# Attention on one core: the softmax sums turned by a third transposition instead of a product with a picking matrix

## The reference

```
a = layernorm(x) @ w_qkv                    # q, k, v of 16 heads, 32 numbers each
scores[q, k] = (q * 32**-0.5) . k           # windows of 128 queries; keys of the window before,
                                            # the same and the next (384; at a sequence's ends 256)
attn = softmax(scores)                      # over the keys
x = x + layernorm(attn @ v)
x = x + layernorm(ffn(layernorm(x)))        # ffn's weights: a base and 8 experts mixed per batch by a gate
```

## Time and profile before

| | |
|---|---|
| median of three runs | 2935.83 us (2935.25 to 2944.34) |
| profiled execution, its own time | 2944.44 us |
| its span, first to last instruction | 2942.7 us |
| mean granted TensorE clock | 0.993 of full speed |
| attention loop's first and last transposition of outputs | 586.2 us, 1301.4 us |
| one round of eight steps (turn of the maxima at 666.04 to that at 709.43) | 43.4 us |

### The profile page before, as it was taken

One profiled execution on the slowest core, in us unless ns is written; L12 is line 12 of the kernel. 1 busy time (PEld: TensorE's weight loads), 2 busy tenths in 40 slices (PEclk: granted clock), 3 DMA queues, 4 the chain that ended last, 5 costly groups with the idle time before them and its releaser, 6 DMA issues.

```text
span 2942.7 us, 55697 instructions
## 1 busy us (share of the span) xinstructions
PE 2878.3 (98%) x20380; PEld 2399.2 (82%) x20380; DVE 1994.3 (68%) x3769; ACT 1733.9 (59%) x3385; POOL 856.6 (29%) x715
## 2 busy tenths in 40 slices
PE   8999999999999999989989999999999999999998
PEld 6888888788888888777867888888888888888886
DVE  5333333488888887778868766886769766786664
ACT  3222222367776766666546666766667666686666
POOL 1000000188888887874400000400005000040003
PEclk9999999999999999999999999999999999999999
DMA  6554555688788879959998866986769765895642
GB/s 215 185 171 171 186 188 193 215 193 197 191 199 197 196 193 219 220 167 393 400 389 327 295 208 221 348 324 204 245 212 404 272 204 201 287 390 201 233 136 86
DMA packets 361430, 697.11 MB, mean 237 GB/s; under 512 B 26576, under 2 KB 127056, under 8 KB 361184
## 3 DMA queue, kind: packets, MB, share of 16 engines
q1 hardware_dynamic: 335456, 629.63, 66.8%
q10 hardware_dynamic: 17424, 32.24, 3.1%
q0 software_dynamic: 8304, 31.98, 2.7%
HBM read 525.45 MB, written 167.78 MB: 236 GB/s over the span
## 4 chain that ended last, share of the span: by engine, by line
PE 86%; DMA 6%; DVE 4%; ACT 2%; issue 1%; POOL 1%; ACTq 0%; SPq 0%; DVEq 0%; POOLq 0%
PE a_acc L577 17%; PE e_hid L1397 8%; PE e_hid L1399 8%; PE e_hid L1398 8%; PE e_acc L1414 8%; PE e_acc L1416 8%; PE e_acc L1415 8%; PE a_ps_score L628 6%; PE a_ps_keys L647 6%; PE a_ps_out L676 5%; DMA a_q_st<-a_max_rows 2%; DMA a_gate_att<-o_scratch 2%; PE a_ps_out L684 2%; DVE a_gate_stats L1665 1%; PE a_turn L572 1%
## 5 line engine op out<-in xcount | busy, mean ns | idle before, releaser
L1787 DVE SCALAR_TENSOR_TENSOR e_part<-e_ring,e_g_cols,e_part 128x512 f32<-128x512 f32 x896 | 644.8, 775 | 5.2 <-DMA e_ring<-mix_rows 2.8
L493 DVE TENSOR_REDUCE a_neg_max<-a_ps_score 128x1 f32<-128x384 f32 (+1 forms) x1024 | 491.6, 527 | 63.0 <-PE a_ps_score L628 51.9
L329 POOL TENSOR_TENSOR a_total<-a_probs 128x512 f32<-128x512 f32 x256 | 323.9, 1282 | 592.4 <-ACT a_probs L421 592.2
L421 ACT ACTIVATE a_probs<-a_ps_keys 128x384 f32<-128x384 f32 (+1 forms) x1024 | 429.6, 477 | 53.9 <-PE a_ps_keys L647 24.2
L1811 DVE TENSOR_TENSOR e_u_lo<-e_u,e_u_hi 128x512 fp32r<-128x512 f32 x256 | 180.6, 706 | 372.0 <-ACT e_u_hi L1545 371.9
L1541 ACT ACTIVATE e_u<-e_hid,e_mb 128x512 f32<-128x512 f32 x256 | 176.9, 691 | 427.7 <-PE e_hid L1399 418.2
L1270 POOL TENSOR_SCALAR e_var<-e_moments 128x4 f32<-128x4 f32 x15 | 6.7, 447 | 1269.6 <-DVE e_moments L1823 1269.0
L628 PE MATMUL a_ps_score<-a_k_st,a_q_st 96*128 96x384 f32 (+1 forms) x1024 | 333.9, 361 | 3.5 <-DMA a_q_st<-qk_scratch 2.5
L647 PE MATMUL a_ps_keys<-a_q_st,a_k_st 97*128 97x384 f32 (+1 forms) x1024 | 314.8, 350 | 12.2 <-DMA a_q_st<-a_max_rows 11.1
L339 POOL TENSOR_TENSOR a_total<-a_total,a_probs 128x512 f32<-128x512 f32 x224 | 286.3, 1280 | 67.0 <-ACT a_probs L421 64.3
L473 DVE TENSOR_TENSOR a_qk<-a_acc,a_qk 128x512 fp32r<-128x512 f32 x128 | 88.1, 690 | 308.1 <-ACT a_qk L370 308.1
(11 more groups left out here) (158 smaller groups left out, 6508.5 us busy)
## 6 DMA issues: line engine op xcount, KB each, us to landing
e_ring<-mix_rows SPq DMA_DIRECT2D x558, 512.0 KB, 5.5
qk_scratch<-a_qk SPq DMA_DIRECT2D x128, 512.0 KB, 3.2
a_k_st<-qk_scratch SPq DMA_DIRECT2D x180, 256.0 KB, 4.4
a_q_st<-qk_scratch SPq DMA_DIRECT2D x180, 256.0 KB, 4.4
v_scratch<-a_v SPq DMA_DIRECT2D x64, 256.0 KB, 3.0
a_v_sb<-v_scratch SPq DMA_DIRECT2D x64, 256.0 KB, 4.9
o_scratch<-a_out SPq DMA_DIRECT2D x128, 128.0 KB, 2.9
x_scratch<-a_gate_x POOLq DMA_DIRECT2D x16, 1024.0 KB, 10.0
```

The source lines that it names most:

```text
L329: add = pool.tensor_tensor(total[:, g % 2, i], p[0], p[1], ALU.add)
L421: act.activation(probs[:, m % PROBS, h, 0:(hi - lo) * WIN], ps_keys[x % TRIO][:, 0:(hi - lo) * WIN], ACT.Exp, scale=SCALE).then_inc(exp_do ...
L493: dve.tensor_reduce(neg_max[:, g % 2, i, h:h + 1], ps_score[y % TRIO][:, 0:(hi - lo) * WIN], AX_X, ALU.max, negate=True).then_inc(reduced, 1)
L1787: dve.scalar_tensor_tensor(out=part[:, n % 2, half, :], in0=ring[:, slot, :], scalar=g_cols[:, b, e:e + 1], in1=so_far, op0=ALU.mult, op1= ...
```

## The change

The third call of `turn_out` becomes a transposition like the two before it, of the whole block of sums, 128 columns into all of part 3 of `ps_turn`. The sums then stand in columns 32 h + i, so the reciprocal reads columns 0 and 1 of each head's 32 and writes them ordered by window and head. `pick`, the two instructions that fill it and their two events go.

```
         neg_max = sb("neg_max", [P, 2, 2, QH], F32)
-        pick = sb("pick", [P, 2 * QH], F32)
-        inv_sum = sb("inv_sum", [P, 2, 2 * QH], F32)
+        inv_sum = sb("inv_sum", [P, 2, 2, QH], F32)
...
-            pool.memset(pick[:, :], 0.0).then_inc(const_done, 1)
-            pool.wait_ge(const_done, 4)
-            pool.affine_select(out=pick[:, :], in_=pick[:, :], compare_op=ALU.not_equal, fill=1.0,
-                               base=0, pattern=[[-1, 2], [-E, QH]], channel_multiplier=1).then_inc(const_done, 1)
-            pool.wait_ge(const_done, 5)
...
-                dve.reciprocal(inv_sum[:, g % 2, :], ps_turn[:, 3, 0:2 * QH]).then_inc(inv_done, 1)
+                dve.reciprocal(inv_sum[:, g % 2], ps_turn[:, 3, :].rearrange("p (h e) -> p e h", e=E)[:, 0:2, :]).then_inc(inv_done, 1)
...
-                                  inv_sum[:, g % 2, :].unsqueeze(2).to_broadcast([P, 2 * QH, E]),
+                                  inv_sum[:, g % 2].rearrange("p w h -> p (w h)").unsqueeze(2).to_broadcast([P, 2 * QH, E]),
...
-                for i in range(2):
-                    pe.transpose(ps_turn[:, 1 + i, :], out_t[:, g % 2, i, :], ident[:, :])
-                pe.matmul(ps_turn[:, 3, 0:2 * QH], out_t[:, g % 2, 2, :], pick[:, :],
-                          start=True, stop=True, skip_group_check=True).then_inc(out_turned, 1)
+                for i in range(3):
+                    mm = pe.transpose(ps_turn[:, 1 + i, :], out_t[:, g % 2, i, :], ident[:, :])
+                mm.then_inc(out_turned, 1)
...
-            pe.wait_ge(const_done, 6)
+            pe.wait_ge(const_done, 4)
```

## The result

The changed kernel takes 2934.88 us in the median of 20 runs (2928.62 to 2940.93). The kernel before, run in turn with it, now takes 2944.27 us in the median of 20 (2935.25 to 2952.83). The ratio is 0.9968, with a 95% interval of 0.9959 to 0.9978: 9.4 us less, between 6.5 and 12.1. The forecast time was 2925.3, with a gain of 10.5. The gain came out nearly as worked out; the time missed by 9.6 us, because the base that it was taken from, the median of three runs, was low. The measured time lies outside the likeliest case's own range (2922.5 to 2929) and just inside the wide one (2918.5 to 2936).

A forecast was written before the change was run, and what follows sets the result against it. TensorE's order was taken to bound the attention loop: 0.111 us less per group, 0.098 per step let through, over 108 of 128 steps 10.6, said 10.5; 2935.83 - 10.5 = 2925.3 us, 8 in 10 between 2918.5 and 2936.

The forecast's parts named there:

- the likeliest case: Attention loop: the cut passes through with a gain of 8 to 13 us, likeliest 2925.3 us, own range 2922.5 to 2929; chance 0.53.
- signs of being wrong: A round of eight steps above 43.1 us or below 42.4, or as forecast with longer waits after 1130 us.
- The step that failed: Final sum: the 10.5 us gain taken from 2935.83 us, the median of three timed runs, giving 2925.3.
- Price of the removed and the added instruction: TensorE, each of 128 groups: picking product occupies 0.222 us, a transposition 0.111; order shorter by 0.111, at most 14.2 us total.
- That a true fp32 product is four passes: Skill rule for the picking product: by it 42.6 us in sum; the prediction used the trace's two load and product pairs.
- What VectorE and ScalarE let through: Reduce 7 and exponential 7: five steps of eight pass 0.111 us, three 0.07, 0.10, 0.06; 0.785 per round, 0.098 per step.
- Rival B: ScalarE holds the attention step because keys 2's delay isn't hidden; gain 5.9 us, 2929.9, or nothing if VectorE holds too; chance 0.20.
- Rival C: Every group gives 0.111 us, steps with DMA waits too: 14.2 us, 2921.6, or 2918.5 without the longest late wait; chance 0.12.
- Steps that give nothing back: Attention steps where TensorE waits for a DMA lose the gain: 20 of 128 taken out, leaving 108 x 0.098 = 10.6 us.
- Rival D: Late waits for the row of maxima grow; if they double, 13.9 us come on top, 2939.2; chance 0.12, two thirds for partial growth.
- VectorE's strided reciprocal, GpSimd, 32 bytes of memory: Side effects taken as 0: reciprocal 0 to 0.05 us, hidden; GpSimd's start 0; buffers moved 32 bytes, bounds -3 to +3 us.
- rival E: TensorE's clock: the third transposition might double the fifth at 1.2 GHz between 1180 and 1230 us; 4.6 us, 2929.9; chance 0.03.

The follow-up runs named there:

- experiment 2: Changed kernel with the block of sums turned twice into the same place, so four transpositions and four weight loads per group; 2941.45 us, ratio 1.0 to the kernel before.
- experiment 4: Kernel before the change, picking product kept but in the one-pass float32 form (F32R), with one load and one product; 2935.04 us, ratio 0.997 to the kernel before.
- experiment 3: Changed kernel without the third transposition, reciprocal reading the second window's block, so the output is not the attention's; 2930.1 us, ratio 0.9956 to the kernel before.
- experiment 5: Changed kernel with the three transpositions moved two products earlier, before scores 6, into TensorE's wait for reduce 3; 2932.76 us, ratio 0.9967 to the kernel before.
- experiment 7: Changed kernel with the transpositions before scores 6 and both rows of maxima sent by SyncE; 2935.66 us, ratio 0.9981 to the kernel before.
- experiment 6: Changed kernel with both rows of maxima sent by SyncE, so ScalarE issues no DMA between exponentials 4 and 5; 2934.87 us, ratio 0.9977 to the kernel before.
- experiment 1: Changed kernel with an unused buffer of 32 bytes per partition where the picking matrix was, so later buffers lie as before; 2932.29 us, ratio 0.9964 to the kernel before.

## Why the prediction was right and where it was wrong

The mechanism and the gain came out as forecast, and none of the prediction's signs of being wrong was seen. The step that failed is the base, and it stands last in the list.

- *Price of the removed and the added instruction* (0.222 and 0.111 us): right. Experiments 2 and 4 show it from both sides, with four loads of two kinds at 43.37 and 43.39 us for a round and three of two kinds at 42.61 and 42.59. The trace alone had it, in the pitch of the loads.
- *That a true fp32 product is four passes* ("FP8 and Floating Point Precision" of the Trainium skill, "TensorE Precision Notes"): the row shows two pairs of load and product for each call, and experiment 2 confirms that their price is that of two loads. With four such pairs one transposition more would not have restored the time of before. What a pair does inside TensorE, no row shows.
- *What VectorE and ScalarE let through* (0.785 us of a round): right, 0.78. Steps of the round that starts at 617.38 us became shorter by 0.117, 0.106, 0.110, 0.113, 0.073, 0.046, 0.107 and 0.109 us, for which I had written 0.111, 0.111, 0.111, 0.111, 0.07, 0.06, 0.111 and 0.10. Rival B is out: the delay of keys 2 was hidden, as its product moved by 0.11. (Rival B's own sum is off: 6 x 0.07 + 0 + 0.07 is 0.49 us for a round, not 0.44, which makes 6.6 us and 2929.2.) Rival C is out as well, by the three steps that gave less. In one place this was luck: the prediction looked at reduce 7 and exponential 7 and not at reduce 6, for which scores 1 waits, and that limit too left room for just this cut. Experiments 3, 5 and 7 ran into it.
- *Steps that give nothing back* (20 of 128): fits. 9.4 us over 0.098 is 96 steps that give, where 108 were forecast; the interval of the gain allows 66 to 123, so the term can't be tested closer than that. Rival D did not happen: 14.2 us of row waits after 13.9. The mechanism exists all the same: with both rows sent by SyncE these waits come to 22.0 and 20.6 us (experiments 6 and 7).
- *VectorE's strided reciprocal, GpSimd, 32 bytes of memory*: nothing, as taken. The reciprocal's median is 0.198 us in both traces; experiment 1 is the memory.
- *The clock* (rival E): the mean granted clock is 0.993 in both profiled executions, with 128 transpositions more, and between 1180 and 1230 us it is 0.97 where it was 0.90. The rule of the Trainium skill ("TensorE: Matmul & The Clock Gate", "Part 4: PE-mode transpose"), that a transposition does not count as activity like a product, shows no effect here; the transpositions stand among other products, so it is not tested either.
- *The step that failed* is the last one, "From the median: 2935.83 - 10.5 = 2925.3". The median of three runs stood 8.4 us below that of 20, 2944.27; the other 1.1 us of the miss are the gain, 9.4 in place of 10.5 and within its interval. The three runs are the first three of the 20, and two of them are the lowest two of all: bad luck in the draw. The prediction had the sign of it in hand: it noted that the profiled execution and one of the three timed runs stood 9 us above the other two, and put that down to waits that differ between executions, but then took the lower pair as the base. From the kernel's own profiled execution the same sum gave 2933.9, which is 1.0 us from the result; that a single execution came so near is luck too, as the 20 runs spread from 2935.25 to 2952.83. That waits for DMAs make the difference is shown in part only: the profiled execution of kernel 2, with the round of the kernel before, took 7.8 us less than that kernel's. 6.2 of them lie in the loop (709.7 us after 715.9), and its loads wait 3.5 us less for rows and for q; the rest stays open. With a base so uncertain the size of the gain (9.4 against 10.5, both about the 8.8 us of the bound that I set) was the only part that could be forecast to a few us.

## What to carry to other kernels

Count the weight loads of a small product, not its columns: here a plain float32 product with a stationary operand of 128 columns loaded it twice, and a transposition or a one-pass form once, at 0.11 us for each load. Before pricing a cut on an engine that is "98% busy", find all instructions of the other engines that the next products wait for, not only the last ones, and read how far each could move; the smallest margin is what the cut is worth, and the next cut of the same size may be worth a sixth of it. And when executions scatter by as much as the gain, forecast the ratio and take the base from all of them, the profiled one included (here 2940.1, still 4 us low).

## What had not been expected

- A DMA issued between two of ScalarE's exponentials holds the second for 0.23 us (pitch 0.60 instead of 0.37), although the transfer is of 2 KB; the issue stands in the trace with 0.58 us.
- Moving SyncE's two sends of 2 KB ahead of its loads of 256 KB cost 26 us (2961.86 against kernel 7's 2935.66); q arrived late 45 times between 590 and 1290 us. The sends are small, but SyncE waits for the maxima before it issues them, and the loads waited with them. The order of one instruction stream, with the same work in it, was the largest lever touched.
- The part of the program behind the loop, the same in all of these kernels, scatters by 7 us between profiled executions. Where that scatter comes from was not tried.
